# Reordering the folds, the mix and the low parts of group 1 in the opening of an adaptive-LoRA, attention and mixture-of-experts kernel

## The reference

```python
# first block: LoRA picked by adapter id, then causal attention over 8 rows of the batch
# (32 query heads, 8 key/value groups), then an output projection
Bx   = einsum('bni,bri->bnr', x, B[ids]);  c = einsum('bnr,bor->bno', Bx, A[ids])
qkv  = einsum('sbh,ph->sbp', c, weight_qkv)        # 8 groups of 4 q, 1 k, 1 v heads
attn = softmax(where(causal, q @ k.T * scale, min))
x    = x + einsum('sbe,he->sbh', attn @ v, weight_proj)
# second block: q, k, v with RMS norms and rotary positions, attention over 512 cached
# and 128 own keys, output projection, then a feed-forward with 2 of 8 LoRA experts
x    = x + ffn(cond2(x, Wq, Wk, Wv, Wo, caches, ...))
```

## Time and profile before

| | |
|---|---|
| median of 3 runs | 1454.23 us |
| the profiled execution | 1452.84 us, its span 1451.1 us |
| TensorE busy | 1426.5 us, 98% of the span |
| VectorE, ScalarE, GpSimd busy | 1194.8, 877.2, 676.0 us |
| mean granted clock of TensorE | 0.997 |
| mean DMA traffic | 103 GB/s |
| DMA traffic between 45 and 89 us | about 204 GB/s |

### The profile page before, as it was taken

The page is one execution under the profiler, slowest core; times in us unless marked ns, Lnnn a source line. Parts: engine busy times, 40 slices in busy tenths (PEclk is TensorE's granted clock), DMA queues, the critical chain, the costliest instruction groups (busy, mean ns, idle before and its releaser), DMA issues.

```text
span 1451.1 us, 26043 instructions
## 1 busy us (share of the span) xinstructions
PE 1426.5 (98%) x8344; PEld 1220.0 (84%) x8344; DVE 1194.8 (82%) x2694; ACT 877.2 (60%) x2272; POOL 676.0 (47%) x966
## 2 busy tenths in 40 slices
PE   8899999989999999999999999999999999999998
PEld 7788888778888888888888888888888888888886
DVE  3788887778888888888888888888889888887866
ACT  3432332356777667767776677677766766766641
POOL 0462322235555555555555555555555555544322
PEclk9999999999999999999999999999999999999999
DMA  7888795234334423442443344334423442321102
GB/s 243 181 206 193 160 205 162 79 92 97 85 87 107 95 66 88 95 100 72 90 109 86 74 95 96 83 80 101 110 69 81 103 95 68 108 62 54 42 17 98
DMA packets 359015, 150.03 MB, mean 103 GB/s; under 512 B 299608, under 2 KB 325464, under 8 KB 358880
## 3 DMA queue, kind: packets, MB, share of 16 engines
q1 hardware_dynamic: 347776, 114.36, 34.3%
q0 software_dynamic: 10240, 33.56, 8.5%
q10 hardware_dynamic: 864, 0.43, 0.1%
HBM read 124.19 MB, written 24.12 MB: 102 GB/s over the span
## 4 chain that ended last, share of the span: by engine, by line
PE 95%; DVE 2%; ACT 1%; issue 1%; DMA 1%; POOLq 0%; POOL 0%; SPq 0%; DVEq 0%
PE ps_o L843 12%; PE ps_t L1086 12%; PE ps_o L845 11%; PE ps_o L844 11%; PE ps_b L843 5%; PE ps_b L845 5%; PE ps_b L844 5%; PE ps_q L844 4%; PE ps_q L845 4%; PE ps_q L843 4%; PE ps_a L843 3%; PE ps_a L844 3%; PE ps_a L845 3%; PE ps_a L915 3%; PE ps_t L875 2%; PE ps_q L937 1%
## 5 line engine op out<-in xcount | busy, mean ns | idle before, releaser
L1596 ACT ACTIVATE sm<-sm,mn 128x640 f32<-128x640 f32 x256 | 211.2, 825 | 212.1 <-DVE mn L2106 210.1
L1965 DVE TENSOR_TENSOR pT_lo<-ps_t,pT_hi 128x512 fp32r<-128x512 f32 x320 | 220.2, 688 | 91.1 <-ACT pT_hi L1508 90.6
L1508 ACT ACTIVATE pT_hi<-ps_t 128x512 fp32r<-128x512 f32 x320 | 188.6, 589 | 39.6 <-PE ps_t L1086 38.8
L1086 PE MATMUL ps_t<-ident,sm 128*128 128x128 f32 x1280 | 196.1, 276 | 3.0 <-ACT sm L1606 1.7
L1086 PEld LDWEIGHTS ps_t<-ident,sm 128*128 128x128 f32 x1280 | 148.2, 140 | 50.3 <-DVE qT_lo L1965 17.0
L731 POOL TENSOR_TENSOR z<-pairs_p,zl 128x128 f32<-128x128 f32 x160 | 57.9, 404 | 168.8 <-DVE pairs_p L1818 168.8
L843 PE MATMUL ps_o<-pT_lo,v_hi 128*128 128x512 f32 x320 | 125.5, 392 | 0.0
L844 PE MATMUL ps_o<-pT_hi,v_lo 128*128 128x512 f32 x320 | 125.2, 391 | 0.0
L845 PE MATMUL ps_o<-pT_hi,v_hi 128*128 128x512 f32 x320 | 124.9, 390 | 0.0
L796 POOL CAST v_hi<-vraw 128x512 fp32r<-128x512 f32 x64 | 42.0, 656 | 176.5 <-PE ps_o L845 176.5
L843 PE MATMUL ps_o<-wo_lo,oT_hi 128*128 128x512 f32 x256 | 117.6, 460 | 2.3
(11 more groups left out here) (266 smaller groups left out, 4256.0 us busy)
## 6 DMA issues: line engine op xcount, KB each, us to landing
fv<-st SPq DMA_DIRECT2D x128, 128.0 KB, 2.4
tab<-tab_scratch SPq DMA_DIRECT2D x64, 256.0 KB, 3.5
wblk<-n_L_attn_weight_qkv_dram SPq DMA_DIRECT2D x24, 384.0 KB, 6.1
wpraw<-_L_attn_weight_proj_dram SPq DMA_DIRECT2D x8, 1024.0 KB, 6.2
kst_scratch<-in_L_cond_k_cache_dram SPq DMA_DIRECT2D x32, 256.0 KB, 5.0
mask<-mask_scratch SPq DMA_DIRECT2D x64, 128.0 KB, 4.0
vst_scratch<-in_L_cond_v_cache_dram SPq DMA_DIRECT2D x32, 256.0 KB, 5.8
wtile<-in_L_cond_Wq_dram SPq DMA_DIRECT2D x112, 64.0 KB
```

The lines of the kernel that those rows point to most:

```text
L1086: mm = pe.transpose(ps_t[bank][:, o * P:(o + 1) * P], i, ident[:])
L1508: act.activation(dst, src, ACT.Copy).then_inc(t_hi, 1)
L1596: act.activation(sm[:, h, :], sm[:, h, :], ACT.Exp, bias=mn[:, h:h + 1], scale=-1.0, accum_out=den[:, h:h + 1]).then_inc(e_done, 1)
L1965: dve.tensor_tensor(lo, src, hi.bitcast(F32), ALU.subtract).then_inc(t_lo, 1)
```

## The change

Nothing is computed otherwise; instructions change their place, in group 1 and just before it.

- TensorE: in group 1, fold 4, fold 5 stand ahead of the two z_groups, and the mix product ahead of z_out(1, 0). Other groups keep their order.
- ScalarE: in group 1 fold_copy stands ahead of the two z_copies.
- VectorE: out_low(0, 3) moves from behind products_s(0, 5) to behind soft_max(0). turn(2) no longer stands ahead of z_low(1, 0); its four transposes are spread: behind x2_sum(1, 0), (1, 1), (1, 2), and behind out_low(1, 0). Other turns stay.

```diff
@@ TensorE
                 if i == 1:
                     p_group(i, 0)
                     p_group(i, 1)
-                z_group(i, 0)
-                fold(i, 4)
-                z_group(i, 1)
-                fold(i, 5)
-                if i >= 2:
+                    fold(i, 4)
+                    fold(i, 5)
+                    z_group(i, 0)
+                    z_group(i, 1)
+                    mix_product(i)
+                else:
+                    z_group(i, 0)
+                    fold(i, 4)
+                    z_group(i, 1)
+                    fold(i, 5)
                     p_group(i, 0)
                 z_out(i, 0)
                 z_out(i, 1)
-                mix_product(i)
+                if i >= 2:
+                    mix_product(i)
@@ ScalarE
+                if i == 1:
+                    fold_copy(i)
                 z_copy(i, 0)
                 z_copy(i, 1)
-                fold_copy(i)
+                if i >= 2:
+                    fold_copy(i)
@@ VectorE
-            def turn(g):
+            def turn(g, cs=range(NC_)):
...
-                for c in range(NC_):
+                for c in cs:
...
             products_s(0, 5)
-            out_low(0, 3)
             sums_s(0, 4)
...
             soft_max(0)
+            out_low(0, 3)
             soft_sum(0)
...
-                if i + 1 < G:
+                if 1 < i < G - 1:
                     turn(i + 1)
                 z_low(i, 0)
                 z_low(i, 1)
...
                 x2_sum(i, 0)
+                if i == 1:
+                    turn(2, [0])
                 x2_sum(i, 1)
+                if i == 1:
+                    turn(2, [1])
...
                 x2_sum(i, 2)
+                if i == 1:
+                    turn(2, [2])
                 products_s(i, 0)
                 products_s(i, 1)
                 sums_s(i, 0)
                 out_low(i, 0)
+                if i == 1:
+                    turn(2, [3])
                 z_low(i, 2)
```

## The result

The changed kernel takes 1457.57 us, the median of 18 runs (1454.53 to 1458.98), against 1454.04 for the kernel before (18 runs, 1452.66 to 1456.09). The ratio is 1.0024, with a 95% interval of 1.0017 to 1.0030: 3.5 us slower. The profiled execution of the changed kernel has a span of 1456.7 us at a mean granted clock of 0.993.

What follows compares the result with a forecast made beforehand. TensorE was taken to bound the kernel (95% of the chain that ended last). A stall of +2.4 us at z_out(2, 0) and +1.5 for the clock gave +3.9, so 1458.1 us for the median; range 1455.4 to 1460.0.

Steps and rivals of the forecast that it cites:

- Parts 1 to 3: Opening: out_low(0, 3) moved, folds and mix ahead of z, turn in pieces; TensorE keeps about 2.4 us.
- part 3: Turn in pieces on VectorE: x2_sum(1, 0) starts at 56.15, scores_s(1, 2) at 60.9; TensorE keeps about 2.4 us.
- Part 4, the signal: SyncE's wait for all four turn pieces: w_turned, and load_w(3) behind it, come 5.45 us later.
- Part 4, the stall: Load, tables and scatters queue behind w_turned; z_out(2, 0) starts at 90.6 instead of 88.20, +2.4 us (+1.8 to +2.9).
- Rival B: Load, tables and scatters overlap in the queue, only SyncE's issue order binds: +0.1 us, 1454.4; chance 0.10.
- Part 5, the clock: After TensorE idles 4.8 us ahead of z_out(2, 0), its clock falls to the lower level: +1.5 us (0.9 to 1.7).
- rival A: Stall at z_out(2, 0) comes, but the clock stays up or falls during the wait: +2.4 us, 1456.6; chance 0.15.
- Rival D: Clock also falls in the opening, behind the 1.2 us hole; z_out(2, 0) later too: +5.5 us, 1459.7; chance 0.12.
- Rival C: Queue makes up more than the delay, so the opening's full gain stands: -2.4 us, 1451.8; chance 0.07.

Runs made afterwards that it cites:

- e1: Changed kernel with SyncE issuing group 1's eight tab_scratch DMAs behind the 16 scatters instead of ahead; ratio to the kernel before 0.9988.
- e2: Kernel before with only the eight tab_scratch DMAs moved behind the scatters; ratio to the kernel before 0.9999.
- e7: Changed kernel with turn(2) put back whole ahead of z_low(1, 0), the other moves kept; ratio to the kernel before 1.0000.
- e10: Changed kernel, unchanged, profiled a second time; one run, z_out(2, 0) 43.75 us after fold(1, 0).
- e9: Kernel before, unchanged, profiled a second time; one run, z_out(2, 0) 43.1 us after fold(1, 0).
- e5: Changed kernel with 14 overwritten identity products on TensorE just ahead of z_out(2, 0); ratio to the kernel before 1.0014.
- e6: Kernel before with SyncE also waiting for x2_sum(1, 2) before load_w(3), signal 5.4 us later; ratio to the kernel before 1.0019.
- e3: Kernel before with SyncE also waiting for out_low(1, 0) before load_w(3), signal 7.2 us later; ratio to the kernel before 1.0037.
- e4: Changed kernel with 28 overwritten identity products on TensorE just ahead of z_out(2, 0); ratio to the kernel before 1.0026.
- e12: e1 with the third piece of turn(2) behind products_s(1, 1) instead of ahead of products_s(1, 0); ratio to the kernel before 0.9984.
- e8: e1 with out_low(0, 3) put back at its old place; ratio to the kernel before 0.9995.

## Why the prediction held, and where it did not

It forecast 1458.1 us and slower; it was 1457.57. The mechanism is the one forecast: the late signal, the queue behind it, the stall at z_out(2, 0), and in one of two profiles the clock. That the size came out within 0.6 us is partly luck. The sum's +3.9 us was to lie at z_out(2, 0) and just behind it; there the two profiles have 2.8 and 0.7, and the rest of the 3.5 between the medians lies elsewhere.

- **Parts 1 to 3, the gain of the opening: right.** z_group(1, 0) behind a hole of 1.13 us (1.2), z_out(1, 0) 2.8 us earlier than before (2.7), a wait of 0.61 us for products_s(1, 0), and e1 keeps 2.4 us of it at z_out(2, 0) (2.4). z_group(1, 1) waited 0.51 for GpSimd, as foreseen; the 0.17 that z_out(1, 2) waited for x2_sum(1, 0) was not. The first part of the prediction took TensorE's hole of 3.54 us for what matters there; e2 and e7 show that it was VectorE's turn ahead of z_low(1, 0), which part 3 moves.
- **Part 4, the signal: right in time.** load_w(3) came 5.3 us later (5.45), directly behind the fourth piece.
- **Part 4, the stall: mis-sized.** z_out(2, 0) came 1.2 us later than before, 0.7 in e10, outside the bounds of 1.8 to 2.9. The term that was too large is the load's: I counted 11.35 us from its issue to the start of the tables' data, the time until the share fell to zero. From 64.13 to about 74.5 it took 10.4, and the window of 385 GB/s starts there. The packets in the traces split the difference in two halves. The load's 128-byte packets ran for 10.0 us before (58.65 to 68.62) and for 9.5 in the changed kernel (65.54 to 75.04); and the first packet for tab_scratch starts at 74.56, 0.5 us before the load's last one ends. Why the load itself ran shorter is open: it took 10.0 us in e2 and e7 and 10.3 in e9, where it goes out early, and 9.2 to 9.5 in the ten profiles that issue it late. The tables' 5.5 us were as counted and the scatters' 10.5 near the 10.7. In all, from load_w(3)'s issue to z_out(2, 0) I had 27.95 us; the changed kernel took 26.8, e10 26.4, e5 27.2, e6 27.1 and e3 27.5. So 3.4 to 4.6 us of delay are hidden, where I found 3.0, and two executions of the same kernel differ by 0.45. Rival B had a grain of truth in that transfers overlap at their ends.
- **Part 5, the clock: right in kind, too sure.** With it the changed kernel is 2.8 us late at group 7, without it 0.7. I put rival A, in which it doesn't fall, at 0.15; the changed kernel fell in one of two profiles, the late signal of e3 in its one, at 92.1 behind 3.49 us. The hole that I took as the sign, 3.54 us in the opening, was followed by a fall within 1.2 us of its end in five of the six profiles that have it, and not in e2.
- **What is left.** 2.8 or 0.7 at group 7 stand against 3.5 in the medians. Behind group 7 the profiles part by other low stretches: one at 276.8 us in the changed kernel, 278.3 in e4, 273.5 in e5, 271.5 in e6 and 274.2 in e9, none there in the others, and one or two between 300 and 328 us in all of them, the kernel before among them. From group 7's first fold to the end of the span the profiles take between 1215.9 and 1217.9 us; the two of the kernel before are at 1215.9 and 1217.3, the two of the changed kernel at 1217.1 and 1217.9. The early stretch at 24 us, 1.6 us each time, may be more frequent with the new order, as said under e9. It would fit that e1, e7 and e12 gain 2.4, 1.1 and 3.0 us at z_out(2, 0) but only 1.2, 0.2 and 2.4 in the medians; but e6, with the old order, loses 1.2 more in the medians than at group 7. More low stretches are not the whole of it: in runs at the same mean granted clock of 0.996 the changed kernel takes 1457.5 us (mean of 7) and the kernel before 1454.7 (mean of 30 beside e1, e5 and e12). How the 3.5 us divide between the wait and these stretches stays open, since the runs don't show their stretches one by one.
- **Small slips in the sums.** 16 issues at 0.63 us are 10.1, not 10.2, and the end of products(1, 0) adds up to 60.82, not 60.85. Neither moves the forecast.
- **Rival D** did not happen in the changed kernel, whose hole was 1.13 us; e8 had it at 1.75. **Rival C**'s full gain came about only once the tables were out of the way.

## What to carry to other kernels

A signal that an engine gives is paid for by whoever is queued behind its waiter: before moving the instruction that raises it, follow the waiting engine's queue to its last member and compare with when that is needed. Here 5.3 us of delay on a weight load that nobody wanted soon held up 16 small DMAs that TensorE wanted. And where a late load cannot be helped, put transfers with no early reader behind those that have one: moving eight DMAs turned a loss of 3.5 us into a gain of 1.2. And look at what an engine would wait for next before filling its idle time: the hole on TensorE was easy to see, but the wait behind it, for VectorE, set the time.

## What the runs showed of the hardware

- In one DMA queue, a later transfer's data begins while the tail of an earlier one runs: in the changed kernel the first packet for tab_scratch starts at 74.56 us and the load's last ends at 75.04; the rate is 198 GB/s up to 74.5 us and 385 from there.
- TensorE's clock fell to its lower level in one of two executions of the same kernel behind idle stretches of 3.29 and 2.85 us, and behind the same idle stretch of 3.54 us in five of six. It also fell where TensorE was idle for at most 1.0 us at a time: at 24 us, behind a stretch with 2.89 of 3.40 us busy, and at 274 to 278 us, behind one with 1.80 of 3.40 busy (changed kernel, e4, e9).
- A fall costs up to 1.7 us, half of what separates these two kernels, or nothing: in the kernel before z_out(1, 0) starts 12.8 us after fold(1, 0) with a fall ahead of it and without. So a comparison of single executions at this scale is worth little. Places counted from a common instruction repeat to 0.02 us where TensorE sets them (43.05 and 43.07 in the two profiles of the kernel before), and to 0.5 us where a DMA does (44.2 and 43.75 in the two of the changed kernel).
